# Another order of the side work in the first layer's pipelined loop, and the router's two Silu activations together

## The reference, cut to what matters

```python
x = x + attention(token_block(x_in, cond))     # first half
x = x + experts(condition(x, ids, cond))       # second half

# token_block: per token, attention among its own 16 heads of 16
kx  = modulated_linear(x, s)                    # 256 -> 256
A   = softmax(einsum('bnhd,bnjd->bnhj', q, k) / 4)
out = modulated_linear(einsum('bnhj,bnjd->bnhd', A, v), s)

# attention: 16 heads, causal, a decaying bias from an outer product of lines
logits = q k^T * scale + incidence * decay^(i-j)
out = softmax(logits) v @ w_out.T

# condition: six branches of x, joined, then two linear layers and a norm
h = ln(ln(x, pw[ids]), cp[ids]);  t = ln(x, tm[ids]);  s = ln(x, ms[ids])
y = ln(silu(concat(h, t, x + .., s) @ W1 + b1) @ W2 + b2, g, be)

# experts: 8 experts, top 2, 80 places each
probs = softmax(y @ Wr + br); pick two; position = cumulative count; scatter rows
```

## Time and profile before

| | us |
|---|---|
| median of three runs | 2894.8 |
| lowest and highest | 2869.67 and 2911.28 |
| the profiled execution, its own time | 2886.88 |
| its span in the profile | 2885.1 |
| from the start to the second iteration | 185.9 |
| the six full iterations | 352.2 to 1684.4 |
| behind the first layer's loop | from about 1977 |

### The profile page before, as it was taken

How to read it: one execution, slowest core, us unless ns; L and a number is a source line. 1 busy time by engine, 2 the same in 40 slices (tenths; PEclk the granted TensorE clock), 3 DMA queues, 4 the chain that set the end, 5 groups by cost and what they waited for, 6 DMA issues and landing times. The chain is left out here.

```text
span 2885.1 us, 33507 instructions
## 1 busy us (share of the span) xinstructions
PE 2188.8 (76%) x11774; PEld 1365.8 (47%) x11774; DVE 1403.1 (49%) x3626; ACT 1043.0 (36%) x2549; POOL 858.8 (30%) x585
## 2 busy tenths in 40 slices
PE   6348878778787878778778879735999587877777
PEld 5224444444454444444444545424777444444444
DVE  2456566565565565664655653421011136363635
ACT  2014445344344344434434435411222151424242
POOL 0345253253254244244335231131000223231412
PEclk9577888788788778778778688766999889999989
DMA  6100020020020020020020020022222301010100
GB/s 225 39 17 1 21 63 1 32 66 1 22 77 1 15 76 8 15 76 8 15 69 15 1 72 17 16 66 95 99 99 99 98 17 49 27 44 31 44 31 15
DMA packets 62593, 128.55 MB, mean 45 GB/s; under 512 B 14564, under 2 KB 39258, under 8 KB 60130
## 3 DMA queue, kind: packets, MB, share of 16 engines
q1 hardware_dynamic: 46570, 76.19, 7.6%
q0 software_dynamic: 15872, 50.35, 6.0%
HBM read 97.04 MB, written 29.46 MB: 44 GB/s over the span
## 5 line engine op out<-in xcount | busy, mean ns | idle before, releaser
L1036 ACT ACTIVATE att_buf<-att_buf,nmin 128x384 f32<-128x384 f32 (+3 forms) x512 | 287.4, 561 | 664.6 <-DVE nmin L1351 634.0
L876 PE MATMUL bank<-kk,qT 32*128 32x512 f32 (+2 forms) x1024 | 333.8, 690 | 80.4 <-DVE nmin L1351 80.2
L703 POOL TENSOR_TENSOR big<-ex_at,kx 128x2048 f32<-128x2048 f32 x64 | 236.4, 3705 | 301.5 <-DVE xt_na L1145 251.6
L903 PE MATMUL bank<-ident,att_buf 128*128 128x128 f32 x1280 | 248.2, 332 | 32.9 <-ACT att_buf L1044 28.1
L649 POOL TENSOR_TENSOR big<-kx 128x1280 f32<-128x1280 f32 x64 | 162.6, 2567 | 248.0 <-ACT kx L975 237.5
L1340 DVE TENSOR_TENSOR att_buf<-bank,wdiag 128x128 f32<-128x128 f32 x384 | 92.6, 283 | 280.4 <-PE bank L881 270.6
L1044 ACT COPY att_buf<-bank 128x384 f32<-128x384 f32 (+3 forms) x512 | 209.6, 409 | 42.6 <-remote 25.9
L917 PE MATMUL bank<-att_buf,vp 128*32 128x128 f32 x2560 | 218.3, 307 | 0.0
L903 PEld LDWEIGHTS bank<-ident,att_buf 128*128 128x128 f32 x1280 | 183.2, 175 | 46.2 <-issue 26.1
L876 PEld LDWEIGHTS bank<-kk,qT 32*128 32x128 f32 x1024 | 111.8, 224 | 172.6 <-DVE nmin L1351 116.8
L712 POOL DMA_INDIRECT buf_d<-nB,sidx x64 | 62.6, 978 | 331.1 <-DVE sidx L1267 314.1
(11 more groups left out here) (342 smaller groups left out, 4028.3 us busy)
## 6 DMA issues: line engine op xcount, KB each, us to landing
ew<-in_eW SPq DMA_DIRECT2D x16, 1024.0 KB
buf_d<-zero SPq DMA_DIRECT2D x8, 640.0 KB, 8.0
er<-buf_d SPq DMA_DIRECT2D x8, 640.0 KB
y_d<-yy SPq DMA_DIRECT2D x8, 640.0 KB, 9.2
xt_na<-in_xT SPq DMA_DIRECT2D x8, 512.0 KB, 3.5
nA<-in_xN SPq DMA_DIRECT2D x8, 512.0 KB, 4.8
x_d<-x SPq DMA_DIRECT2D x8, 512.0 KB, 3.4
kf<-x_d SPq DMA_DIRECT2D x8, 512.0 KB, 3.3
```

Of the source, the lines that this page charges most:

```text
L703: pool.tensor_tensor(pv[:, c * P:(c + 1) * P, :].rearrange("p (h d) o -> p o h d", d=DH), spread(ex[:, t, :, 8 * c:8 * c + 8], 3, DH), spr ...
L876: pe.matmul(bank[u % 2][:, 0:n], qT[r:r + 32, g, i * P:(i + 1) * P], kk[r:r + 32, g, T * i * P:T * i * P + n], start=True, stop=False)
L903: mm = pe.transpose(bank[3 + u % 2][:, j * P:(j + 1) * P], pr[:, u % NPR, j * P:(j + 1) * P], ident[:])
L1036: act.activation(pr[:, u % NPR, 0:n], pr[:, u % NPR, 0:n], ACT.Exp, scale=-1.0, bias=nmin[:, u % 4:u % 4 + 1], accum_out=rsum[:, i, h:h + ...
```

## The change

The table's numbers change, some pieces get a slot of their own, and GpSimd's list is reordered. Steps before and after (a step is half of the slot, rounded down):

| piece | engine | step before | step after |
|---|---|---|---|
| h1, second half, and kx | VectorE | 0 (h1 first) | 0 (kx first) |
| moments of h1; square root | VectorE; ScalarE | 0; 0 | 1; 1 |
| t turned; copied | TensorE; ScalarE | 0; 1 | 1; 1 |
| h2: normalisation, affine halves | VectorE | 1, 2, 2 | 2, 3, 4 |
| h turned; copied | TensorE; ScalarE | 4; 4 | 5; 5 |
| the eight sums of products | VectorE | 2, 3, 4, 5, 6, 7, 8, 9 | 3, 4, 5, 6, 7, 8, 9, 10 |
| softmax: maximum, subtraction, exponential, sum | VectorE, ScalarE | 9, 9, 10, 10 | 11, 12, 12, 13 |
| reductions of the product with the values | VectorE | 13 to 25 | 14 to 25 |
| u in groups | TensorE | 2 groups in each of 7 to 14 | 3, 3, 2, 3, 3, 2 in 7 to 12 |
| Silu | ScalarE | 11 and 15 | 14 and 14 |
| y | TensorE | 15 and 16 | 15 and 16 |
| y out of its bank; moments; square root; normalisation | VectorE, ScalarE | 17; 17; 18; 18 | 17; 18; 18; 19 |
| affine of f, halves; turn; copy | VectorE; TensorE; ScalarE | 19, 19; 20; 20 | 20, 21; 21; 21 |
| r; out; exponential; sum | TensorE, VectorE, ScalarE | 21, 22; 22; 23; 23 | 22, 23; 24; 24; 25 |
| picks; positions; places | VectorE, TensorE | 24, 24; 25; 26 on | 25, 26; 27; 28 on |
| rows to scatter | VectorE | 28 | 30 |
| token output: turn; copy; product; out | TensorE, ScalarE | 27; 28; 28, 29; 29, 30 | 28; 28; 29, 30; 29, 30 |
| sums of the first half: copy; broadcast; divide | ScalarE; TensorE; VectorE | 18; 19; 19 | 19; 20; 21 |

The diff, cut (of its many lines that only replace a number by a name of the table, two stand here):

```diff
-AT = {"var1": -5, "z": -4, "h1": -3, "h1b": 0, "var2": 1, "kx": 0, "h2": 3,
...
+      "sums": (6, 8, 11, 12, 14, 16, 18, 20), "full": 22, "sub": 24, "ex": 25, "den": 27, "pv": 28, "norm": 54,
...
 pool.tensor_tensor(tt, tt, gb[:, :, 3 * D:4 * D], ALU.add).then_inc(s("tt_ok"), 1)
+pool.wait_ge(s("h1_ok"), 1)
+gather(a["ms"], gac, 2)
 if b1 is not None:
     pool.wait_ge(s("kx_dup"), 1)
     products(0)
-pool.wait_ge(s("h1_ok"), 1)
-gather(a["ms"], gac, 2)
-if b1 is not None:
-    products(1)
 for t in range(T):
     pool.wait_ge(s(f"gath{t}"), 48)
 pool.tensor_tensor(ss, nA[:], ss, ALU.mult).then_inc(s("pool_own"), 1)
 pool.wait_ge(s("pool_own"), 2)
 pool.tensor_tensor(ss, ss, gac[:, :, D:2 * D], ALU.add).then_inc(s("ss_ok"), 1)
+if b1 is not None:
+    products(1)
...
-                                            if n % 2:
-                                                yield AT["u"] + 8 * o + n + 1
+                                            if n in (2, 5, 7):
+                                                yield AT["u"] + 6 * o + 2 * (2, 5, 7).index(n) + 2
...
                                     for o in range(K2):
-                                        yield AT["u"] + 7 + 8 * o
+                                        yield AT["silu"]
...
-                                    if u == N // 2 + 6:
+                                    if u == N // 2 + 8:
                                         broadcast_sums(0)
...
-                                    if u == N // 2 + 4:
+                                    if u == N // 2 + 6:
                                         sums_out(0)
...
-                                    if u == N // 2 + 6:
+                                    if u == N // 2 + 10:
                                         divide(0)
```

76 lines of the change are left out of this document (40 added, 36 removed).

## The result

The changed kernel takes 2711.8 us (median of 4 runs, 2708.3 to 2723.9), the kernel before beside it 2885.3 us (2869.7 to 2911.3). The ratio is 0.9408, 95% interval 0.9365 to 0.9451: 5.9% faster. The forecast of 2777 us had the direction and the mechanism, and its range of 2710 to 2862 us holds the time only at its lower end: 110 us of gain were forecast and 172.5 us came, by the two profiled executions (2886.9 and 2714.4 us).

The account below looks back on a forecast made before the run. No engine was full; engines waited for one another in turn. Terms summed to 19.5 us, less 3, so 16.5 per full iteration: 99 us over six, plus 11 elsewhere, 110 off 2886.9 us gives 2777 us, range 2710 to 2862.

Parts of the forecast that it names:

- the three signs that would show the prediction wrong: TensorE's nmin waits as long at other steps; new two-input VectorE operations at 2.5 us or more; iteration's end on scatters.
- The activations: Pairing the Silus in step 14 ends the second layer's wait and slow half: 5 us an iteration, bounds 0 and 8.
- GpSimd's order with the softmax: Steps 7 to 14: products(2) starts 5 us sooner, VectorE's waits go; 7.5 us an iteration, bounds 0 and 10.7.
- the lock: VectorE and GpSimd exclude one another on SBUF; new hits at h2's halves, f1 to f3 cost 2.5 us above old.
- The t piece: Moving kx ahead and moments and t to step 1 ends a 2.64 us wait: 2 us, bounds -1 and 3.6.
- The router's late part: Steps 17 to 26: spreading the work ends pauses of 3.10 and 3.11 us: 3.5 us, bounds -2 and 8.
- The token output: Turn and products one step later end waits of 3.10 and 2.32 us: 4 us, bounds -2 and 8.
- The end: End of iteration: last indices move to step 30, scatters and x1 arrive together; cost 0, bounds 0 and 2 us.
- The discount of 3 us: Taken off the 19.5 us sum because each term supposes the next engine is ready at once, leaving 16.5 us.
- Other waits: Rival: pauses come up a step later, a third of the gain is left, 5 us an iteration; 2853 us, chance 0.17.
- The lock as a loss on the whole: Rival: VectorE loses up to 12.5 us to GpSimd, stops cost TensorE's clock; 2959 us, chance 0.05.
- The scatters as the end: Rival: scatters become the last thing, every gain in steps 28 to 31 is lost, 4 us; 2801 us, chance 0.16.

Follow-up runs that it names:

- silu_back: Changed kernel with the two Silu activations apart again, first-layer matmul pieces in twos and the second layer one slot later, as before: 2777.0 us, ratio 0.9639.
- g_first: Changed kernel with one move, GpSimd forming the products of the first 128 tokens ahead of issuing the gather of the third rows: 2718.9 us, ratio 0.9471.
- order_back: Changed kernel with GpSimd's order of operations from before the change, all slots as changed: 2734.2 us, ratio 0.9481.
- early_back: Changed kernel with the router's early part (first and second normalisation, turns of second and third source) at its old slots: 2746.0 us, ratio 0.9511.
- f_later: Changed kernel with the turn of the router's input at slot 44 for 43, its copy at 45, router's product at 46 and 47: 2708.6 us, ratio 0.9376.
- late_back: Changed kernel with all that stands behind the second layer, from third normalisation to token output, at its old slots: 2830.9 us, ratio 0.9814.
- fill: Changed kernel with 32 unused transpositions of the identity added on TensorE at slots 38, 40 and 42: 2707.9 us, ratio 0.9385.
- best1: Changed kernel with f_later's and g_first's moves, three token-output sums later, later product sums and GpSimd's addition to xN moved: 2624.1 us, ratio 0.9094.
- rows_early: Changed kernel with the places of the second choice and the rows one step earlier (rows at slot 58 for 60): 2770.7 us, ratio 0.9601.
- all_three: Kernel best1 with the places of the second choice and the rows one step earlier, as in rows_early: 2673.2 us, ratio 0.9261.

## Why the prediction came out as it did

**The mechanism held.** Waits of TensorE in the first layer were the reserve; each one named at the earlier trace rows shrank, from 4.26 to 1.31 us, from 2.64 to none, from 3.10 and 2.32 to 0.72 and none. Of the marks named ahead, the single load, the two halves at 1.99 us, L1223's successor at 0.19 us and no wait of VectorE for products over 1 us appeared. A full iteration took 197.7 us, not 205. The granted clock of one reached 0.84 to 0.85, where 0.85 or more was the mark. But the three signs that would show the prediction wrong appeared as well: a wait for nmin of 8.00 us at another step, affine operations of 3.58 and 3.24 us, and an iteration whose end hangs on the scatters (3.29 us of waiting for their landing). Each cost what is told below, and the pauses that ended gave more.

**Term by term, for a full iteration** (table of stretches; forecast against measured, in us):

- The activations, 5: steps 14 to 17 gave 9.7, but 3.4 of it is work of the first layer that moved ahead of step 14. By silu_back the part is worth 5.4 in steps 3 to 17, as priced. The wait and slow half were priced at 6.05 and gave 4.7, since 1.31 us of the wait stayed. What the term missed is behind step 17, where undoing it lost 5.8 more to the clock.
- GpSimd's order with the softmax, 7.5, less the lock, 2.5: steps 3 to 14 lost 1.8 instead of gaining 5, or gained 1.6 without the 3.4 of work that moved in. Steps 7 to 14 of the prediction's count came down by 10.1 (35.3 us), almost the whole bound of 10.7, and VectorE's wait of 7.24 us went. It did not go for the reason given: the third products start 2.0 us later in the iteration than before, not 5 sooner, and VectorE comes to them later still. In g_first and order_back, where VectorE isn't held, it waits for products again (5.47 and 3.87 us). The normalisation lost 8.8 us in the run of 9.8 us of GpSimd's operations, and the second half of h2's affine 1.4 us. This step failed: I looked for the hits at h2's two halves and counted one operation of GpSimd for each. The hit came at the normalisation, and a run without a gap held VectorE for nearly its whole length.
- The t piece, 2: steps 1 to 3 gave 3.3, and early_back 3.7 in step 1, at the upper bound of 3.6. The steps ahead of it lost 0.7, which no term had.
- The router's late part, 3.5: 3.4. The wait at f was forecast as 1.5 us and measures 4.67 us, since both affine operations were locked (3.58 and 3.24 us for 1.2); f_later shows that it costs no time.
- The token output, 4: steps 27 to 31 gave 10.8; late_back loses 13.3. The second product, 2.0 us, moved behind step 31, so the fair measure is from step 27 to the end: 10.4, above the bound of 8, and 11.1 in late_back. This is the term that was mis-sized most. The two waits were worth 5.4 less 0.7 us. But all of TensorE's work from step 28 to 31 ran at a lower granted clock, 0.69 before and 1.00 after (the row of before is below, that of after above). The turn, the scores and turned units behind it and the first product, the same work in both, took 9.3 us before and 5.0 after: 4.3 us, where the forecast had 1.8 for the slow product alone.

```profile
975.70:997.60 21.90, 15.82 (x64) 7.73 (x64) 6.81 (x31) 6.61 (x21) 7.78 (x8) 0.69 0.14 48
```

- The end, 0: a loss of 0.4. The scatters land 1.8 us behind what x1 would allow, inside the bounds of 0 and 2; that the end lost no more is the clock again, with the last product at 3.72 us for 5.41.
- The discount of 3 us had no ground.

Over the six full iterations the mean gain is 24.3 us against 16.5: six times 7.8, or 47 us of the 62 us missed. The iteration without a router gave 15.4 us for 5 and the one without tokens 17 for 6.

**The main cause behind the sizes** is the clock. The prediction said that a pause is paid for twice and then counted the second payment for the piece right behind it only. In the iteration TensorE's busy time fell by 14.1 us with unchanged work. The two are not to be added blindly, as fill shows: the level matters where TensorE is the bound (steps 23 and 24, 8.8 or 13.3 us; the first scores, 3.5 us) and is free where VectorE is.

Nor are the parts to be added up from the runs that undo them. order_back, silu_back, late_back and early_back lose 22, 65, 119 and 34 us, 240 us for a change that gave 173. Each of them loses 5.5 to 5.8 us an iteration in steps 17 to 27, in three of them without an edit there: a loss that comes only once, though each of these runs shows it. The changed kernel has it too in its first full iteration (54.0 us), and g_first is free of it in its last (49.0 us). No run shows what decides between the two, so that the changed kernel has the shorter stretch in five of its six full iterations has to be called luck.

**The rivals.** Other waits: the new one of 8.0 us is such a wait, worth 6.5 us in step 3, and it was more than paid for. The lock as a loss on the whole: it was there, 13.6 us of VectorE by best1's measure against the 12.5 us of the rival, but the pauses gave more than supposed. The scatters as the end: true of the mechanism, and 1.8 us in size, not every gain of steps 28 to 31.

**Open** is why ScalarE and TensorE stood still in rows_early. That the place of the scatters causes it is shown by best1; that their traffic delays the loading of instructions is only argued from releasers that read remote and issue. Open too is when the lower level ends, on which 4.5 us of an iteration hang in steps 23 and 24.

## What to carry to other kernels

Price a wait of TensorE by the granted clock of all the steps behind it, as far as TensorE bounds them; here 2.95 us more of waiting cost 5.4 us (silu_back, steps 3 to 17) and 4.25 us more cost 11.1 (late_back, from step 27 on), while a wait of 4.67 us cost nothing where VectorE was the bound (f_later). Before comparing a stretch in two kernels, see which pieces crossed its bounds. When work of GpSimd is put one piece behind another without a gap, look for every SBUF-to-SBUF operation of VectorE that comes due in the whole run, small normalisations too, and put a DMA issue between (g_first), or the operations ahead. After such a change read the trace once more: best1 took half as much again out of the kernel by moving the pieces that the change had brought together.

## What the runs showed of the hardware

A VectorE tensor_scalar with one SBUF input (and per-row factors) was held by GpSimd's tensor_tensor as the affine operations were: one of four took 7.1 us, another 2.5 us, beside three operations back to back. VectorE's masked scores, which read PSUM, and its reductions kept their lengths beside the same products. The Trainium skill, "SBUF — State Buffer", section "Who interferes with whom", counts tensor_scalar, in its two-port forms, among the operations that can contend with GpSimd, and tells of the exclusion for the length of an instruction; in these rows it lasted for a run of three. GpSimd's issue of a gather (four of 0.95 us) held nothing: the normalisation took 1.43 us beside it.

Scatters two slots earlier than in the changed kernel made the iteration of the table 5.2 us (rows_early) and 6.6 us (all_three) longer at its end, with standstills of engines that take no part in them (3.3 and 4.1 us in rows_early); scatters at the slots of before, four slots earlier (late_back), and at the changed ones did not.
